# Setup of a decoder kernel: two row loads and the gate scalar stand earlier in the load queue, and the other rows count on a semaphore of their own

## The reference

```python
x = _layernorm(x + _L0_attn_ref(x, L0_attn_w_q, ..., L0_attn_w_o, L0_attn_b_o))      # 16 heads of 128, causal
x = _layernorm(x + _L0_xattn_ref(ctx_512, x, L0_xattn_Wq, L0_xattn_Wk, L0_xattn_gamma_raw))
x = _layernorm(x + _L0_ffn_ref(x, L0_ffn_weight, L0_ffn_scale, ...))                 # 32 masked experts
x = _layernorm(x + _L1_attn_ref(x, ...))                                             # rotary attention
x = _layernorm(x + _L1_xattn_ref(x, ctx_512, L1_xattn_W_k, L1_xattn_b_k, L1_xattn_ln_gamma, L1_xattn_ln_beta))
x = _layernorm(x + _L1_ffn_ref(x, ...))                                              # 16 experts, top 4

# in _L0_xattn_ref
gamma = jax.nn.sigmoid(gamma_raw)                  # the gate scalar
return (1.0 - gamma) * adj_raw + gamma * A_learned
# in _L1_xattn_ref
kv = k_v @ W_k.T + b_k                             # b_k is the key bias, 64 values
```

## Time and profile before

| | us |
|---|---|
| three runs of the kernel | 970.29, 971.85, 972.61 |
| their median | 971.85 |
| the profiled execution, its own time | 972.34 |
| its span, first to last instruction | 970.6 |
| mean granted TensorE clock in it | 0.965 of full speed |

### The profile page before, as it was taken

One profiled execution on the slowest core, in us unless ns is written; L12 is line 12 of the kernel. 1 busy time (PEld: TensorE's weight loads), 2 busy tenths in 40 slices (PEclk: granted clock), 3 DMA queues, 4 the chain that ended last, 5 costly groups with the idle time before them and its releaser, 6 DMA issues. The chain is left out here.

```text
span 970.6 us, 15802 instructions
## 1 busy us (share of the span) xinstructions
PE 888.1 (92%) x4982; PEld 750.7 (77%) x4982; DVE 674.3 (69%) x1869; ACT 410.8 (42%) x1173; POOL 492.3 (51%) x399
## 2 busy tenths in 40 slices
PE   7889999999998669999968999999997689999995
PEld 5678888888887557777746888888886468888885
DVE  3696786786685679888876677677673755555555
ACT  4263553554565121111025666566664632223222
POOL 4766665755511242223335665555550238777773
PEclk8999999999999779999989999999999889999998
DMA  6221121122000331221000111101100001111111
GB/s 185 66 87 38 51 87 49 40 88 73 15 23 1 107 111 48 67 71 31 1 27 1 49 51 49 49 1 50 50 23 18 17 12 53 45 49 49 49 38 44
DMA packets 48106, 47.58 MB, mean 49 GB/s; under 512 B 4833, under 2 KB 39601, under 8 KB 48049
## 3 DMA queue, kind: packets, MB, share of 16 engines
q1 hardware_dynamic: 48048, 46.87, 15.5%
HBM read 45.81 MB, written 1.05 MB: 48 GB/s over the span
## 5 line engine op out<-in xcount | busy, mean ns | idle before, releaser
L826 ACT ACTIVATE a_probs<-bank,a_neg_peak 128x128 f32<-128x128 f32 (+1 forms) x256 | 103.4, 430 | 90.3 <-DVE a_neg_peak L934 90.3
L1390 DVE SCALAR_TENSOR_TENSOR b_acc<-bank,b_gate,b_acc 128x256 f32<-128x256 f32 x256 | 111.5, 479 | 14.0 <-PE bank L1301 8.0
L1300 PE MATMUL bank<-b_w,xt_hi 128*128 128x512 f32 x256 | 103.2, 403 | 1.5 <-DVE b_acc L1390 1.4
L1301 PE MATMUL bank<-b_w,xt_lo 128*128 128x512 f32 x256 | 101.6, 397 | 0.0
L854 ACT ACTIVATE a_probs<-a_probs,a_row_inv 128x128 f32<-128x128 f32 (+1 forms) x256 | 91.9, 447 | 19.0 <-DVE a_row_inv L942 19.0
L934 DVE CUSTOM_DVE_ANT_0 bank<-bank,causal 128x128 f32<-128x128 f32 (+1 forms) x256 | 82.4, 394 | 15.6 <-PE bank L696 15.2
L832 ACT ACTIVATE a_probs_t<-bank 128x512 f32<-128x512 f32 x96 | 53.9, 596 | 77.0 <-PE bank L716 77.0
L1505 POOL TENSOR_TENSOR d_h_lo<-d_h,d_h_hi 128x512 fp32r<-128x512 f32 x40 | 51.8, 1297 | 52.7 <-ACT d_h_hi L1624 39.2
L1710 DVE TENSOR_TENSOR d_h<-d_silu,bank 128x512 f32<-128x512 f32 x40 | 27.5, 688 | 73.0 <-PE bank L113 72.9
L735 PE MATMUL bank<-a_probs_t,a_vals 128*128 128x256 f32 x256 | 76.5, 380 | 0.0
L1258 POOL TENSOR_TENSOR b_masked<-b_raw,tern 128x1024 bf16<-128x1024 f32 x16 | 34.3, 2150 | 81.4 <-PE bank L1289 81.4
(11 more groups left out here) (267 smaller groups left out, 2575.7 us busy)
## 6 DMA issues: line engine op xcount, KB each, us to landing
b_raw<-_L_ffn_expert_masks_dram SPq DMA_DIRECT2D x32, 256.0 KB, 2.9
d_raw<-in_L_ffn_we_dram SPq DMA_DIRECT2D x48, 128.0 KB, 2.2
a_raw_k<-in_L_attn_w_k_dram SPq DMA_DIRECT2D x8, 512.0 KB, 6.5
a_raw_q<-in_L_attn_w_q_dram SPq DMA_DIRECT2D x8, 512.0 KB, 5.7
a_raw_v<-in_L_attn_w_v_dram SPq DMA_DIRECT2D x8, 512.0 KB, 7.3
a_raw_o<-in_L_attn_w_o_dram SPq DMA_DIRECT2D x8, 512.0 KB, 3.6
a_raw_q<-in_L_attn_Wq_dram SPq DMA_DIRECT2D x8, 512.0 KB, 4.6
a_raw_o<-in_L_attn_Wo_dram SPq DMA_DIRECT2D x8, 512.0 KB, 3.6
```

Source lines behind the costliest of these rows:

```text
L826: nc.scalar.activation(probs[s % 2][:, i, at:at + width], c.banks[i][:, at:at + width], ACT.Exp, bias=neg_peak[:, n:n + 1], scale=-1.0, ac ...
L1300: nc.tensor.matmul(out, c.xt_hi[:, k, cols], w[j][:, k], start=k == 0, stop=False)
L1301: last = nc.tensor.matmul(out, c.xt_lo[:, k, cols], w[j][:, k], start=False, stop=k == KC - 1)
L1390: last = nc.vector.scalar_tensor_tensor(acc[e][:, t], c.banks[t % RING][:, e * D:(e + 1) * D], g, acc[e][:, t], ALU.mult, ALU.add)
```

## The change

The two loads of the key bias and the gate scalar's load move ahead of the mask and of `ffn_weight`, directly behind the four weight groups. The key bias loads get the semaphore `s_key_bias`, and VectorE waits for these two alone before L312. The other four rows count on `c.s_rows`, a semaphore that lives on after `setup`; GpSimd waits for it before the one instruction in `attention` of layer 0 that first reads one of them. Each load has the same size and form as before.

```diff
-        s_ctx, s_w, s_const, s_bias, s_rows = (c.sem(f"su_{n}") for n in ("ctx", "w", "const", "bias", "rows"))
+        s_ctx, s_w, s_const, s_bias, s_key_bias = (c.sem(f"su_{n}") for n in ("ctx", "w", "const", "bias", "key_bias"))
...
                 weights.first_loads(sp)
+                sp.dma_start(c.rows[:, ROW_BK, 0:DC], a["L1_xattn_b_k"].partition_broadcast(P)).then_inc(s_key_bias, 16)
+                sp.dma_start(c.rows[:, ROW_BK, DC:P], a["L1_xattn_b_k"].partition_broadcast(P)).then_inc(s_key_bias, 16)
+                sp.dma_start(g_raw[:], a["L0_xattn_gamma_raw"].partition_broadcast(P)).then_inc(s_bias, 16)
                 sp.dma_start(causal_f[:], a["causal"]).then_inc(s_bias, 16)
                 sp.dma_start(c.ffn_weight[:], a["L0_ffn_weight"].rearrange("(k p) i -> p k i", p=P)).then_inc(c.s_ffn_weight, 16)
-                sp.dma_start(g_raw[:], a["L0_xattn_gamma_raw"].partition_broadcast(P)).then_inc(s_bias, 16)
-                sp.dma_start(c.rows[:, ROW_BK, 0:DC], a["L1_xattn_b_k"].partition_broadcast(P)).then_inc(s_rows, 16)
-                sp.dma_start(c.rows[:, ROW_BK, DC:P], a["L1_xattn_b_k"].partition_broadcast(P)).then_inc(s_rows, 16)
                 for r, n in ((ROW_BO, "L0_attn_b_o"), (ROW_SCALE, "L0_ffn_scale"), (ROW_GAMMA, "L1_xattn_ln_gamma"), (ROW_BETA, "L1_xattn_ln_beta")):
-                    sp.dma_start(c.rows[:, r], a[n].partition_broadcast(P)).then_inc(s_rows, 16)
+                    sp.dma_start(c.rows[:, r], a[n].partition_broadcast(P)).then_inc(c.s_rows, 16)
...
-                dve.wait_ge(s_rows, 6 * 16)
+                dve.wait_ge(s_key_bias, 2 * 16)
...
+                    pool.wait_ge(c.s_rows, 4 * 16)
                     nc.gpsimd.tensor_tensor(c.x[:], c.x[:], c.rows[:, ROW_BO].unsqueeze(1).broadcast_to([P, NT, D]), ALU.add).then_inc(s_residual, 1)
```

More of the change, by code:

```diff
@@ L93, in decoder @@
         c.ffn_weight, c.clipped, c.tern = sb("ffn_weight", [P, KC, D]), sb("clipped", [P, KC, D]), sb("tern", [P, KC, D], BF16)
-        c.s_ffn_weight = c.sem("ffn_weight")
+        c.s_ffn_weight, c.s_rows = c.sem("ffn_weight"), c.sem("rows")
         c.gamma, c.one_less = sb("gamma", [P, 1]), sb("one_less", [P, 1])
```

## The result

| | before | changed kernel |
|---|---|---|
| median of 12 runs each | 972.18 | 968.17 |
| lowest and highest | 970.29, 973.91 | 963.54, 970.52 |
| ratio, 95% interval | | 0.9952 (0.9938 to 0.9966) |

The account below looks back on a forecast made before the run. The end of setup was taken as the bound: VectorE reaches the barrier last, at 24.96, after idling for the beta row. Barrier 1.79 + clock 1.5 - late k load 0.1 = 3.19 us; predicted 969.0, range 967.8 to 970.9.

Parts of the forecast that it names:

- The wait: End of setup: VectorE idles 4.34 us before L312 for the beta row, which L312 does not read.
- Where the stall goes: Barrier ending setup: ScalarE becomes last at 23.17, so the barrier moves 1.79 us from 24.96, not 4.34.
- The forecast sum: Whole kernel: 1.79 barrier + 1.5 clock - 0.1 late k load = 3.19 us.
- The moved loads: Setup's loads: moving the key bias forward is worth nothing, as it lands by 18.7 anyway; bounds 0 and 0.1 us.
- The cover of 1.3 us: Setup, ScalarE's mask: landing by 18.7 against need at 19.98; beyond that, each microsecond would go straight to the barrier.
- The rule on completion order: Setup's loads: completion is not first in, first out, so the key bias could land late; then 971.85, chance 0.06.
- The clock: First projections after setup: TensorE's pause shrinks from 2.75 to 0.95 us, the clock stays up, 1.5 us back.
- the forecast's second case: First projections: the clock falls all the same, only 1.79 us remains, 970.55 or 970.06; chance 0.27.
- The late k load: Start of attention: the second k weights land at 29.45, GpSimd could start at 29.36, so 0.1 us is lost.
- Reaching the end: From the first projections to the kernel's end: the earlier start carries through, 3.19 us in sum.
- The shift is rigid: After TensorE's pause at 41.91: engines wait for each other and for loads issued on their signals, so the shift persists.
- the third rival of the prediction: Later joins, as at 311.7: one more stretch falls to the low clock, losing about 2.8 us, 973.3; chance 0.05.

Follow-up runs that it names:

- e1: Changed kernel with the loads back in the old order, only the semaphores split: 0.9968 of before, 3.1 us under, median 969.75.
- e4: Changed kernel plus three idle TensorE matmuls behind the last similarity: 0.9963 of before, 3.6 us under, median 969.52.
- e7: The changed kernel once more, unaltered, a second set of 12 runs: 0.9967 of before, 3.2 us under.
- e8: Changed kernel with the second group's k weights loaded inside setup instead of at the start of attention: 0.9958 of before, 4.1 us under.
- e2: Changed kernel with only the loads moved, VectorE still waiting for all six before the kv adds: 0.9986 of before, 1.4 us under.
- e3: Kernel before plus ten idle TensorE matmuls behind the last similarity, filling the pause at the barrier: 0.9992 of before, 0.8 us under.
- e11: Changed kernel with the second group's k load inside setup and three idle matmuls behind the last similarity: 0.9950 of before, 4.9 us under.
- e5: Kernel before plus six idle TensorE matmuls in each of its two pauses inside setup: 1.0007 of before, 0.7 us slower.
- the first set: The changed kernel's first 12 runs against the kernel before: ratio 0.9952, 4.7 us under, median 968.17.
- e6: Changed kernel plus six idle TensorE matmuls in each of its two pauses inside setup: 0.9965 of before, 3.4 us under.
- e9: Changed kernel plus twelve idle matmuls in setup's pauses and the second group's k load inside setup: 0.9984 of before, 1.6 us under.
- e10: e9 plus nine more idle TensorE matmuls behind the last similarity: 0.9955 of before, 4.4 us under, median 967.12.

## Why the prediction was right and wrong

**The wait.** Right. VectorE waited for a row that it does not read; the semaphore alone (e1) brings 3.1 us, and L312 is released by TensorE.

**Where the stall goes.** Right in kind: the barrier is set by ScalarE's `sim` tail, and L111 starts 0.3 us behind it. The term's size is the step that failed: "so nothing pulls this end forward. The barrier thus moves from 24.96 to 23.17: **1.79 us**, not 4.34". In the profiled pair L111 moved by 3.03 us. 23.17 was read from one execution in which the clock was low twice inside `setup`. In the kernel before that was harmless, because the row landed at 23.16 in any case; I took it for a property of the program, and gave this term no bounds where the others had some. The profiles without idle work inside `setup` fall into two kinds: last similarity at 22.4 to 22.75, with the clock low near 8 to 11 us (before, e1, e4, e7, e8), and at 21.0 to 21.3 without that stretch (changed, e2, e3, e11). ScalarE's `sim` ends at 23.1 to 23.4 in the five and at 21.7 to 21.9 in the four. The changed kernel keeps the difference. L111 starts at 23.36 to 23.70 in e1, e4, e7 and e8, and at 22.14 to 22.22 in e11 and the changed kernel, while the three kernels that wait for the beta row where it was have it at 25.12 to 25.57 (before, e3, e5). In the slower kind the forecast fits: e8 has L111 at 23.51 and the scores at 30.19, against 23.5 and 30.2. The term is 1.6 to 1.9 us in that kind and 3.0 to 3.1 in the faster; with both about equally frequent in nine profiles, an estimate of 2.4. The forecast sum becomes 2.4 + 1.5 - 0.24 = 3.7, inside both intervals. The mis-sized term thus accounts for 0.6 of the 1.5 us by which the forecast fell short of the first set; the rest, like the difference between the two sets (4.7 and 3.2), is within their noise, and no run assigns it. How often each kind of `setup` comes was not measured, and what brings it stays open.

**The moved loads.** "Worth nothing here" fits the changed kernel, where e1's time doesn't differ clearly, and was wrong as a statement on the loads: "The four rows land at 23.2, as before, because the same bytes are ahead of them" failed by 1 us (22.2), and e2 gains what that gives. The mask landed later, as supposed: issued at 10.69, 7.7 us to landing, 18.39, and ScalarE, done with the instruction before it at 18.29 (17.98 + 0.31), began L267 at 18.44. The cover of 1.3 us that I had counted was used up, by the mask's later landing and by the quicker `setup`. It still cost nothing, since ScalarE then had 1.02 us to wait for the first similarity. So that a late mask "would go straight to the barrier" was wrong too: the first microsecond of it is covered by that wait. In e6, with a faster `setup`, ScalarE did wait for the mask, for 0.85 us, and GpSimd still ended later.

**The rule on completion order** (the Trainium skill, "DMA: Bandwidth & Descriptors", queues, rings and completion order) did not come to bear: in the changed kernel the key bias, the gate scalar, the mask, `ffn_weight` and the rows landed in the order of issue, 15.7 to 22.2.

**The clock.** Right in place and size: 1.49 us in the profiled pair, 1.48 from before to e3, 1.5 from e9 to e10. These are all readings of traces; in time e3 alone shows nothing clear. Behind pauses at this barrier of 0.30 to 0.96 us the clock stayed at 1.00 in seven profiles; behind 2.61, 2.75, 3.00 and 5.59 it was at 0.50; behind 1.91 (e3) and 2.45 (e6) it was not. At this barrier the low stretch goes with the longer pauses, it is absent where idle matmuls filled a part of the pause (e3, e10), and the forecast's second case did not come in any profile with a short pause. "0.95 is nearer to these two than to 2.75" came true, but the length of the pause alone is not what decides. TensorE also pauses inside `setup`, ahead of the second half of the x transposes and ahead of the first products. Behind the first of these pauses the clock was at 0.50 after 1.38 us (e7) and at 1.00 after 2.04 (changed). The second, 1.91 to 2.27 us, was followed by a stretch at 0.50 in all nine profiles without idle work there. The Trainium skill ("TensorE: Matmul & The Clock Gate", section "Why this matters for your kernels") warns only of longer gaps than those of 2.61 and 2.75 us, behind which the clock was at 0.50 here, and the measurement decides. The Trainium skill's remark in the same page, in its Part 1, that the number of slow matmuls varies between runs of one kernel fits what `setup` showed, and I had applied it only to the term that it would shrink.

**The late k load.** Right in kind: GpSimd waited for it, and by e8 it came 0.24 us late, against 0.1 forecast. Whether that lateness reaches the end, as the forecast had it, no run shows.

**Reaching the end.** In the profiled pair 4.52 us at the scores are 4.2 at the end of the span (970.6 and 966.4). That is partly luck: from the first scores to the end the thirteen profiles took between 933.6 and 941.0 us, so in single executions more happens on the way than in the whole change (last section). "The shift is rigid" was too strong.

**The range.** 967.8 to 970.9 held the median of the changed kernel's runs, 968.17, but not 0.9952 of the time before, about 967.2 from the median that was given. With 2.4 for the barrier term the same sum gives 968.2.

## What to carry to other kernels

When a semaphore counts loads that one reader doesn't need, split it; the gain is not the wait but the distance to the next engine at the barrier, so list the end of each engine there. Ask, too, whether that next engine's end is fixed or varies from execution to execution: a wait on a load that lands at nearly the same time in every execution hides such variation, and once it is gone, the gain depends on the execution. One profile of the kernel before gives one draw of that end, so give the term bounds. And price the pause of TensorE as well as the delay: shortening a pause of 2.75 us gave back 1.5 us of clock here, speeding TensorE up in front of a barrier that GpSimd sets took the same 1.5 us away in e9's profile, and with a pause of 5.59 us the scores came 2.65 us later behind L111 than at the full clock (9.33 against 6.68).

## What the runs showed that I had not expected

**The same pause is followed by either clock.** At the end of layer 0's attention TensorE pauses for 3.41 to 3.44 us in all thirteen profiles. Windows over the same piece of the program, first of before, then, with the pause ahead of it, of e1, which is 3.2 us ahead there:

```profile
311.80:318.60 6.80, 5.61 (x25) 5.37 (x26) 5.62 (x12) 2.91 (x9) 0.00 (x0) 0.50 0.01 2
```

```profile
306.38:309.81 3.43, 0.00 (x1) 0.05 (x2) 1.91 (x5) 3.43 (x13) 0.00 (x0) 1.00 0.00 0
308.60:315.40 6.80, 5.33 (x41) 5.01 (x42) 5.62 (x12) 4.35 (x12) 0.00 (x0) 1.00 0.01 2
```

In e1 the clock stayed up through the pause and behind it, and 41 matmuls started where 25 did. The same happened in e8; in the other eleven profiles, the changed kernel's among them, it was at 0.50 to 0.54 in the 3 us behind the pause. It is the third rival of the prediction with the sign open: such stretches help as well as hurt. What decides them in an execution was not tried.

**A load in layer 1 lands late in some executions.** GpSimd near 545 us, in the timelines of before and of e4:

```profile
546.63 0.62 POOL L391 TENSOR_TENSOR a_wk_hi<-a_raw_k,one 128x256 fp32r<-128x256 f32 x1 [5.49 <-DMA a_raw_k<-in_L_attn_Wk_dram]
```

```profile
545.41 0.62 POOL L393 TENSOR_TENSOR a_wk_hi<-a_raw_k,one 128x256 fp32r<-128x256 f32 x1 [7.08 <-DMA a_raw_k<-in_L_attn_Wk_dram]
```

The load was issued at 542.12 in before and at 539.32 in e4: 4.4 and 6.0 us to landing, for the same 128 KB. TensorE's scores then wait 1.98 us instead of 0.44. e1, e3, e6 and e9 had the long one as well (5.9 to 6.1 us), the other eight the short one (4.3 to 4.5). In e3 and e6 a stretch at the lower clock followed. e3's profiled execution, 1.61 us ahead of before at the first scores, is level with it at 552.87 and 2.2 us behind at the end, which accounts for its 974.57. These two effects are of the size of the change, and so a likely part of why 12 runs of this kernel place the gain no better than between 3.3 and 6.0 us.
